# Moving two value products and the transposed maxima within each attention slot

## The chip, the core and the metric

The kernel runs on one core of a Trainium2 chip. The metric is device time in microseconds (us). Three runs of the kernel before took 499.0, 501.17 and 502.9 us (median 501.17). The profiled execution took 502.17 us, of which 500.3 us are the span that the profile covers.

## What is computed

Four batches of 512 tokens with 256 features go through a cross-attention block and then a mixture of eight experts. The attention has 16 heads of 16 features; with the causal mask only the first 512 context rows matter. The change touches the attention alone:

```python
Q = (query @ Wq.T + bq).reshape(B, Sq, H, dk).transpose(0, 2, 1, 3)
K = (key @ Wk.T + bk).reshape(B, Sk, H, dk).transpose(0, 2, 1, 3)
V = (value @ Wv.T + bv).reshape(B, Sk, H, dk).transpose(0, 2, 1, 3)
scores = jnp.einsum('bhqd,bhkd->bhqk', Q, K) / jnp.sqrt(jnp.float32(dk))
scores = jnp.where(causal, scores, -jnp.inf)
attn = jax.nn.softmax(scores, axis=-1)
out = jnp.einsum('bhqk,bhkd->bhqd', attn, V)
```

After the output projection and the residual, the feed-forward block picks two of eight experts per token and adds a shared expert. That part is not changed.

## The kernel before, in words

The program is written out engine by engine: five instruction streams, joined by semaphores, in an order that was fixed by hand. The attention works in **slots**, one for a group of four heads of a batch: 16 slots in all. The first slot has an order of its own (FIRST), then a loop runs three batches of four slots, and the last batch is written out with three slots.

A slot for head group g mixes four kinds of work on TensorE, in the order of the list SLOT. In an entry the number is that of a part.

- **R 0 to 5** (lines 624 and 626): scores of the *next* group with queries on partitions, each with a small mask product. They go to the two bank pairs of set_a. VectorE takes the row maxima from each (line 1306), and after R 5 it splits the maxima into three bfloat16 parts with four small instructions (lines 1312 to 1318).
- **MAX** (line 634): the transposed maxima of the next group, four small products from those parts into a bank of set_b. ScalarE copies the 12 rows out (line 995, function max_rows) and issues a small DMA (line 1038) that puts them beside the queries, where the next slot's S products find them.
- **S 0 to 10** (line 644): scores of *this* group with keys on partitions, already reduced by the maxima. S 0 to 3 belong to the first 128 keys, S 4 to 7 to the second, S 8 and 9 to the third, S 10 to the last. ScalarE takes the exponential of each (line 1074) into the buffers pT, and GpSimd masks the diagonal block of each key tile (line 528).
- **PV 0 to 3** (line 654): the product of the *previous* group's probabilities with the values, one part for each key tile, added up in the fourth bank of set_b. Four heads run side by side in column strips of the array. When PV 3 is done, ScalarE copies the sum out (line 995, function p_v).

Two rules set who waits. The S products and MAX share three banks of set_b in turn, so each of them may start only when the job three places before it has been read by ScalarE. The R products share two bank pairs, so each may start only when VectorE has finished with the R job two places before it. ScalarE reads the banks in the same order as TensorE fills them; p_v and max_rows stand in its stream ahead of exponential number MAX_AT.

Slots come in two kinds. In a **projection slot** (the first and third of each batch in the loop) TensorE first projects queries and keys for the next batch (line 675), VectorE first adds the biases (line 1254), and ScalarE and GpSimd split the projected values into bfloat16 parts; ScalarE does the second pair of these copies after exponential 7 (part2). In a **plain slot** (the second and fourth) none of this happens. After the fourth slot TensorE transposes the result, projects the next values and applies the output projection.

Of the kernel before, what the change touches and what calls it, by code (L numbers as in the profile page):

```python
# [44 lines left out]
def build(nc, x, ctxT, wqT, bq, wkT, bk, wvT, bv, woT, bo, gwT, wupT, wdnT, sgT, suT, sdT, out):  # L45
    B, S, D = x.shape
# [33 lines left out]
    with ExitStack() as ctx:  # L80
# [209 lines left out]
        def heads_in_bank(k):  # L290
# [21 lines left out]


        SLOT = [("R", 0), ("PV", 0), ("R", 1), ("PV", 1), ("R", 2),
                ("S", 0), ("R", 3), ("S", 1), ("R", 4), ("S", 2), ("S", 3), ("R", 5), ("S", 4), ("S", 5),
                ("S", 6), ("S", 7), ("PV", 2), ("PV", 3), ("S", 8), ("MAX", 0), ("S", 9), ("S", 10)]

        assert A_ALL % 2 == 0
        MAX_AT = 9
        FIRST = [("R", 0), ("R", 1), ("R", 2), ("S", 0), ("R", 3), ("S", 1), ("R", 4), ("S", 2), ("R", 5)]  # L320
        FIRST += [(kind, n) for kind, n in SLOT if kind == "MAX" or kind == "S" and n > 2]
        for order in (SLOT, FIRST):
# [139 lines left out]
        def _(pool):  # L462
# [38 lines left out]
            def pool_turn(signal, count):  # L501

                pool.wait_ge(signal, count)
                pool.sem_inc(pool_turns)
# [12 lines left out]
            def mask_group(n, last=False, split=None):  # L517
# [3 lines left out]
                for k in range(QT):  # L521
# [3 lines left out]
                    jobs = sum(job[0] <= k for job in S_JOBS)  # L525
                    pool_turn(b_free, n + jobs + (1 if jobs > MAX_AT and not last else 0))
                    diag = pT[k][:, :, 0:P]
# [75 lines left out]
        def _(pe):  # L603
# [25 lines left out]
            def maxima(n, par, g_count, first=False):  # L629
                pe.wait_ge(mparts_ready, g_count)  # L630
                if not first:
                    pe.wait_ge(b_free, n - 2)
                for k in range(QT):
                    last = mm(bank(par)[0:3 * HG, k * P:(k + 1) * P],
                              mparts[:, k].rearrange("p i h -> p (i h)"), identb[:], start=True, stop=True)
                last.then_inc(b_full, 1)

            def scoresT(g, j, n, par):
                pe.wait_ge(b_free, n - 2)
                k, h0, heads = S_JOBS[j]  # L640
                w = S - k * P
                for i in range(heads):
                    h = g % 2 * HG + h0 + i
                    last = mm(bank(par)[:, i * w:(i + 1) * w], kstack[0:ROWS + 3, g // 2, h, k * P:(k + 1) * P],  # L644
                              qstack[0:ROWS + 3, g // 2, h, k * P:S], start=True, stop=True)
                last.then_inc(b_full, 1)
# [63 lines left out]
            def slot(g, count, n_b, par_b, rows=None, projection=None, wait_rows=None, order=SLOT):  # L710
# [9 lines left out]
                for kind, j in order:  # L720
# [4 lines left out]
                    elif kind == "S":  # L725
                        if j == 0 and order is FIRST:
                            pe.wait_ge(b_free, B_GRP0)
                        if j == 0:
                            pe.wait_ge(max_in, DMA * (count + 1))
                        skip = 1 if rows and j >= MAX_AT else 0  # L730
                        scoresT(g, j, n_b + j + skip, par_b + j + skip)
                    elif kind == "MAX" and rows:
                        maxima(n_b + MAX_AT, par_b + MAX_AT, count + 2)

# [259 lines left out]
        def _(act):  # L994
# [38 lines left out]
            def max_rows(n, par, g):  # L1033
                act.wait_ge(b_full, n + 1)
                copy(mrows[0:3 * HG, :], bank(par)[0:3 * HG, :]).then_inc(b_free, 1)
                act.wait_ge(b_free, n + 1)
                h = g % 2 * HG
                nc.scalar.dma_start(qstack[ROWS:ROWS + 3, g // 2, h:h + HG, :], mrows[0:3 * HG, :]
                                    ).then_inc(max_in, DMA)
# [24 lines left out]
            def exps(n, par, pv=None, rows=None, split=None, down={}):  # L1064


                for j, (k, h, heads) in enumerate(S_JOBS):
                    if pv and j == MAX_AT:
                        p_v(*pv)
                    if rows is not None and j == MAX_AT:  # L1070
                        max_rows(n, par, rows)
# [17 lines left out]
            def p_v(g, count):  # L1089
                act.wait_ge(pv_full, count + 1)  # L1090
                copy(oT[:, g, :], pv_bank).then_inc(pv_free, 1)
# [553 lines left out]
```

## Time and profile before

| | |
|---|---|
| Runs | 499.0, 501.17, 502.9 us |
| Profiled execution | 502.17 us, span 500.3 us |
| TensorE busy | 458.4 us, 92% of the span |
| VectorE busy | 308.2 us, 62% |
| ScalarE busy | 210.1 us, 42% |
| GpSimd busy | 193.1 us, 39% |
| Chain that ended last | TensorE 68%, VectorE 10%, ScalarE 9%, DMA 6% |
| Mean granted TensorE clock | 0.982 of full |

The busy times are read against the span; a busy TensorE includes the tail of each matmul after its last column has been fed. In the timeline rows below the first number is the start, the second the time that the row's instructions cover, and the bracket at the end, where there is one, the idle time of the engine just before the row and what ended it. The next row's start is the better measure of what a piece of work costs in a stream.

### The profile page before, as it was taken

Reading aid. Unit: us, or ns where it says so; the run is one execution under the profiler, and the core shown is the slowest. Engines: PE = TensorE matmul, PEld = TensorE weight load, DVE = VectorE, ACT = ScalarE, POOL = GpSimd, SP = SyncE. Lnnn points to the kernel's source line nnn. Section 1 sums busy time; section 2 is a strip of 40 time slices with the busy share of each in tenths; the row PEclk is TensorE's granted clock in tenths of the full one; section 3 lists DMA queues with packets and bytes.
Section 4 is the critical chain, followed back from the end, with each engine's and each line's share of the span. In section 5 each row is a group of like instructions: output and inputs, shape, how many; then the busy total and the mean of one; then the engine's idle time right before and its main releaser. Section 6 shows DMA issues by size and latency. Waiting matters only on the chain.

```text
span 500.3 us, 10299 instructions
## 1 busy us (share of the span) xinstructions
PE 458.4 (92%) x3154; PEld 318.9 (64%) x3155; DVE 308.2 (62%) x651; ACT 210.1 (42%) x420; POOL 193.1 (39%) x204
## 2 busy tenths in 40 slices
PE   7868999999999999988699799999999999999993
PEld 6644344654447443554256366599999999999852
DVE  4984757477563757656674796855554554555436
ACT  2254666517572566517862352523322322322210
POOL 4123545114541336201512002126666766665420
PEclk9998999999999999999979899999999999999998
DMA  8593322422124121400298900014344344444279
GB/s 263 102 229 107 108 72 65 149 65 73 64 78 145 33 95 47 138 28 2 77 371 292 367 2 21 21 33 65 64 74 74 63 71 70 70 65 74 33 197 338
DMA packets 45574, 53.84 MB, mean 108 GB/s; under 512 B 7760, under 2 KB 41872, under 8 KB 44912
## 3 DMA queue, kind: packets, MB, share of 16 engines
q1 hardware_dynamic: 34320, 39.77, 24.8%
q0 software_dynamic: 7488, 10.31, 12.8%
q10 hardware_dynamic: 3744, 3.47, 2.7%
q8 instruction: 13, 0.21, 0.2%
q14 instruction: 9, 0.07, 0.1%
HBM read 27.09 MB, written 13.67 MB: 81 GB/s over the span
## 4 chain that ended last, share of the span: by engine, by line
PE 68%; DVE 10%; ACT 9%; DMA 6%; issue 5%; SPq 1%; DVEq 0%; ACTq 0%; POOLq 0%
PE set_a L624 7%; PE set_b L654 7%; PE set_a L924 6%; PE set_a L925 5%; PE set_a L923 5%; ACT attention L1074 5%; PE set_a L851 5%; PE set_a L675 4%; PE set_b L644 4%; DVE attention L1306 3%; PE set_b L861 3%; PE set_b L942 3%; PE set_a L832 3%; PE set_b L943 3%; PE set_b L944 3%
## 5 line engine op out<-in xcount | busy, mean ns | idle before, releaser
L1306 DVE TENSOR_REDUCE attention<-set_a 128x2 f32<-128x1024 f32 (+2 forms) x96 | 95.9, 1042 | 28.0 <-PE set_a L626 26.1
L1074 ACT ACTIVATE attention<-set_b 128x512 f32<-128x512 f32 (+1 forms) x176 | 88.4, 570 | 58.5 <-PE set_b L644 45.8
L528 POOL TENSOR_SCALAR_AFFINE_SELECT attention<-attention 128x512 f32<-128x512 f32 x64 | 40.8, 650 | 110.4 <-ACT attention L1074 110.4
L588 POOL DMA_INDIRECT sum_rows<-moe,token_of x39 | 61.8, 1585 | 43.9 <-issue 28.9
L644 PE MATMUL set_b<-attention 99*128 99x512 bf16 (+3 forms) x256 | 60.4, 310 | 13.6 <-ACT attention L1074 10.2
L624 PE MATMUL set_a<-attention 96*128 96x512 bf16 (+3 forms) x256 | 61.5, 306 | 5.6 <-DVE attention L1306 5.4
L580 POOL DMA_INDIRECT e_x<-normed_rows,token_of x39 | 39.4, 1010 | 63.7 <-DVE token_of L1504 37.3
L1173 ACT ACTIVATE moe<-set_a 128x384 f32<-128x384 f32 x39 | 19.1, 490 | 104.9 <-PE set_a L925 104.9
L1529 DVE TENSOR_TENSOR moe<-set_a,moe 128x384 f32<-128x384 f32 x39 | 21.8, 558 | 62.7 <-ACT moe L1173 62.7
L624 PEld LDWEIGHTS set_a<-attention 96*128 96x128 bf16 x256 | 25.3, 99 | 45.3 <-DVE attention L1306 18.0
L923 PE MATMUL set_a<-wup_hi,e_xT_hi 128*128 x156 | 53.1, 340 | 0.0
L924 PE MATMUL set_a<-wup_lo,e_xT_hi 128*128 x156 | 52.9, 339 | 0.0
L925 PE MATMUL set_a<-wup_hi,e_xT_lo 128*128 x156 | 52.8, 338 | 0.0
L626 PE MATMUL set_a<-maskb,identb 128*128 128x128 bf16 x256 | 49.6, 222 | 0.0
L654 PE MATMUL set_b<-attention 128*32 128x128 f32 (+3 forms) x512 | 46.2, 463 | 0.4 <-ACT attention L995 0.3
L644 PEld LDWEIGHTS set_b<-attention 99*128 99x128 bf16 x256 | 19.6, 99 | 37.2 <-ACT attention L1074 24.8
L942 PE MATMUL set_b<-w_down_hi,e_hT_hi 128*128 x117 | 36.4, 311 | 1.3 <-DVE moe L1541 0.8
L995 ACT ACTIVATE attention<-set_b 12x512 bf16<-12x512 f32 (+4 forms) x48 | 25.7, 596 | 22.6 <-PE set_b L820 10.2
L509 POOL TENSOR_TENSOR attention<-attention 128x512 f32<-128x512 f32 x14 | 15.9, 1154 | 47.5 <-ACT attention L995 27.8
L944 PE MATMUL set_b<-w_down_hi,e_hT_lo 128*128 x117 | 32.9, 281 | 0.0
L943 PE MATMUL set_b<-w_down_lo,e_hT_hi 128*128 x117 | 32.9, 281 | 0.0
L995 ACT ACTIVATE attention<-attention 128x512 bf16<-128x512 f32 x32 | 19.4, 644 | 30.9 <-DVE attention L1254 26.2
(167 smaller groups left out, 843.5 us busy)
## 6 DMA issues: line engine op xcount, KB each, us to landing
attention<-attention SPq DMA_DIRECT2D x182, 64.0 KB, 2.6
wup<-in_wupT SPq DMA_DIRECT2D x2, 3072.0 KB, 14.6
sum_rows<-attention SPq DMA_DIRECT2D x2, 2048.0 KB, 13.6
wup<-sum_rows SPq DMA_DIRECT2D x8, 512.0 KB, 7.0
attention<-in_ctxT SPq DMA_DIRECT2D x7, 512.0 KB, 6.2
w_down<-in_wdnT SPq DMA_DIRECT2D x3, 1024.0 KB, 5.0
x_res<-in_x SPq DMA_DIRECT2D x4, 512.0 KB, 7.1
out<-x_res ACTq DMA_DIRECT2D x8, 256.0 KB, 4.0
```

The source lines that it names most:

```text
L588: g.indirect_dma_start(acc[i], bass.IndirectOffsetOnAxis(token_of[:, t:t + 1], 0), e_y[:, t % 2, :], None, compute_op=ALU.add).then_inc(ad ...
L624: mm(dst, qstack[0:ROWS, g // 2, h, k * P:w], kstack[0:ROWS, g // 2, h, 0:w], start=True, stop=False)
L626: last = mm(dst[:, k * P:w], identb[:], maskb[:], start=False, stop=True)
L644: last = mm(bank(par)[:, i * w:(i + 1) * w], kstack[0:ROWS + 3, g // 2, h, k * P:(k + 1) * P], qstack[0:ROWS + 3, g // 2, h, k * P:S], sta ...
L654: last = mm(pv_bank[32 * h:32 * h + 32, k * P:S], vaug[:, k, HG * g + h, :], pT[k][:, h, :], start=k == 0, stop=k == QT - 1, tile_position ...
L923: mm(dst, e_xT_hi[:, a, c, :], wup_hi[:, c, cols], start=c == 0, stop=False)
L924: mm(dst, e_xT_hi[:, a, c, :], wup_lo[:, c, cols], start=False, stop=False)
L925: last = mm(dst, e_xT_lo[:, a, c, :], wup_hi[:, c, cols], start=False, stop=c == C - 1)
L942: mm(dst, e_hT_hi[:, a, m, :], wdn_hi[:, m, cols], start=m == 0, stop=False)
L943: mm(dst, e_hT_hi[:, a, m, :], wdn_lo[:, m, cols], start=False, stop=False)
L1074: nc.scalar.activation(pT[k][:, h:h + heads, :], bank(par)[:, 0:heads * (S - k * P)], ACT.Exp).then_inc(b_free, 1)
L1306: v.tensor_reduce(dst, src, AX.X, ALU.max, negate=True).then_inc(a_free, 1)
```

## The change

The list SLOT is reordered. PV 2 goes from behind S 7 to behind S 0, PV 3 to behind S 1, and MAX from behind S 8 to ahead of it. MAX_AT goes from 9 to 8, which moves p_v and max_rows in ScalarE's stream ahead of exponential 8. FIRST is built from SLOT and so gets the new place of MAX too. No instruction is added or removed.

```diff
         SLOT = [("R", 0), ("PV", 0), ("R", 1), ("PV", 1), ("R", 2),
-                ("S", 0), ("R", 3), ("S", 1), ("R", 4), ("S", 2), ("S", 3), ("R", 5), ("S", 4), ("S", 5),
-                ("S", 6), ("S", 7), ("PV", 2), ("PV", 3), ("S", 8), ("MAX", 0), ("S", 9), ("S", 10)]
+                ("S", 0), ("PV", 2), ("R", 3), ("S", 1), ("PV", 3), ("R", 4), ("S", 2), ("S", 3), ("R", 5), ("S", 4), ("S", 5),
+                ("S", 6), ("S", 7), ("MAX", 0), ("S", 8), ("S", 9), ("S", 10)]
 
         assert A_ALL % 2 == 0
-        MAX_AT = 9
+        MAX_AT = 8
```

The first place is TensorE's stream in the first half of a slot, before the change. L644 is an S product, L624 with L626 an R product, and the rows begin with S 0; the next to last row is the first product of R 4.

```order
L644 MATMUL set_b<-attention 128x512
L617 REGISTER_ALU
L624 MATMUL set_a<-attention 128x384
L626 MATMUL set_a<-maskb,identb 128x128
L624 MATMUL set_a<-attention 128x384
L626 MATMUL set_a<-maskb,identb 128x128
L639 REGISTER_ALU
L644 MATMUL set_b<-attention 128x512
L617 REGISTER_ALU
L624 MATMUL set_a<-attention 128x256
L626 MATMUL set_a<-maskb,identb 128x128
```

The same place with the change:

```order
L644 MATMUL set_b<-attention 128x512
L652 REGISTER_ALU
L654 MATMUL set_b<-attention 32x256 x4
L617 REGISTER_ALU
L624 MATMUL set_a<-attention 128x384
L626 MATMUL set_a<-maskb,identb 128x128
L624 MATMUL set_a<-attention 128x384
L626 MATMUL set_a<-maskb,identb 128x128
L639 REGISTER_ALU
L644 MATMUL set_b<-attention 128x512
L652 REGISTER_ALU
L654 MATMUL set_b<-attention 32x128 x4
```

PV 2 (32x256) now stands between S 0 and R 3, PV 3 (32x128) between S 1 and R 4.

The second place is TensorE's stream from S 7 to the end of the slot, before the change; L634 is MAX.

```order
L644 MATMUL set_b<-attention 128x384
L652 REGISTER_ALU
L654 MATMUL set_b<-attention 32x256 x4
L652 REGISTER_ALU
L654 MATMUL set_b<-attention 32x128 x4
L639 REGISTER_ALU
L644 MATMUL set_b<-attention 128x256 x2
L630 REGISTER_ALU
L632 REGISTER_ALU
L634 MATMUL set_b<-identb,attention 12x128 x4
L639 REGISTER_ALU
L644 MATMUL set_b<-attention 128x256 x2
```

With the change:

```order
L644 MATMUL set_b<-attention 128x384
L630 REGISTER_ALU
L632 REGISTER_ALU
L634 MATMUL set_b<-identb,attention 12x128 x4
L639 REGISTER_ALU
L644 MATMUL set_b<-attention 128x256 x2
L639 REGISTER_ALU
L644 MATMUL set_b<-attention 128x256 x2
L639 REGISTER_ALU
L644 MATMUL set_b<-attention 128x128 x4
```

MAX now follows S 7 directly, and S 8, S 9 and S 10 come after it.

The third place is ScalarE's stream in a projection slot, from exponential 7 on, before the change. The rows of L995 are, in this order, the two copies of part2, p_v (128x512 out of set_b) and max_rows (12x512).

```order
L1074 ACTIVATE attention<-set_b 128x384
L1016 ISA
L995 ACTIVATE attention<-attention 128x512
L1016 REGISTER_ALU
L995 ACTIVATE attention<-attention 128x512
L1073 REGISTER_ALU
L1074 ACTIVATE attention<-set_b 128x512
L1090 ISA
L995 ACTIVATE attention<-set_b 128x512
L1034 REGISTER_ALU
L995 ACTIVATE attention<-set_b 12x512
L1038 DMA attention<-attention 3x4x512
```

With the change:

```order
L1074 ACTIVATE attention<-set_b 128x384
L1016 ISA
L995 ACTIVATE attention<-attention 128x512
L1016 REGISTER_ALU
L995 ACTIVATE attention<-attention 128x512
L1090 ISA
L995 ACTIVATE attention<-set_b 128x512
L1034 REGISTER_ALU
L995 ACTIVATE attention<-set_b 12x512
L1038 DMA attention<-attention 3x4x512
L1073 REGISTER_ALU
L1074 ACTIVATE attention<-set_b 128x512
```

Exponential 8 went behind p_v, max_rows and the DMA issue.

## Rows read from the trace of the kernel before

**Rows 1.** Stretches: length, busy of PE, PEld, DVE, ACT, POOL, clock, DMA, GB/s.
```profile
69.36:83.16 13.80, 13.01 (x95) 5.78 (x93) 8.03 (x12) 8.60 (x18) 8.04 (x8) 1.00 0.15 51
```

**Rows 2.** Waits of PE from 40 to 205 us: total, times, longest.
```profile
PE set_b L644 <- ACT attention L1074: 5.3, 17, 0.6
PE set_a L624 <- DVE attention L1306: 1.0, 6, 0.2
```

**Rows 3.** Timeline of PE, first half of a projection slot.
```profile
76.41 0.38 PE L644 MATMUL set_b<-attention 99*128 99x512 bf16 x1
76.78 0.34 PE L624 MATMUL set_a<-attention 96*128 96x384 bf16 x1
...
77.23 0.38 PE L644 MATMUL set_b<-attention 99*128 99x512 bf16 x1
77.64 0.28 PE L624 MATMUL set_a<-attention 96*128 96x256 bf16 x1
...
78.33 0.59 PE L644 MATMUL set_b<-attention 99*128 99x512 bf16 x2
78.77 0.22 PE L624 MATMUL set_a<-attention 96*128 96x128 bf16 x1
```

**Rows 4.** Timeline of PE, end of that slot; 81.00 from a narrower window.
```profile
80.54 0.86 PE L654 MATMUL set_b<-attention 128*32 128x256 f32 x16
81.00 0.40 PE L654 MATMUL set_b<-attention 128*32 128x128 f32 x8
81.33 0.39 PE L644 MATMUL set_b<-attention 99*128 99x256 bf16 x2
81.65 0.39 PE L634 MATMUL set_b<-identb,attention 128*12 128x128 bf16 x4
...
82.93 0.40 PE L644 MATMUL set_b<-attention 99*128 99x128 bf16 x4 [0.57 <-ACT attention L1074]
```

**Rows 5.** Timeline of DVE in that slot: maximum of R 4, last split.
```profile
78.53 1.23 DVE L1306 TENSOR_REDUCE attention<-set_a 128x4 f32<-128x1024 f32 x1
...
81.12 0.17 DVE L1318 TENSOR_TENSOR attention<-attention 128x16 bf16<-128x16 f32 x1
```

**Rows 6.** Timeline of ACT in that slot, in narrow windows.
```profile
80.83 0.54 ACT L1074 ACTIVATE attention<-set_b 128x384 f32<-128x384 f32 x1
81.20 1.19 ACT L995 ACTIVATE attention<-attention 128x512 bf16<-128x512 f32 x2
82.24 0.64 ACT L1074 ACTIVATE attention<-set_b 128x512 f32<-128x512 f32 x1
82.72 0.65 ACT L995 ACTIVATE attention<-set_b 128x512 f32<-128x512 f32 x1
83.19 0.57 ACT L995 ACTIVATE attention<-set_b 12x512 bf16<-12x512 f32 x1
```

**Rows 7.** Timeline of PE, then of DVE, in the plain slot ahead of it.
```profile
63.81 0.38 PE L644 MATMUL set_b<-attention 99*128 99x512 bf16 x1
64.36 0.28 PE L624 MATMUL set_a<-attention 96*128 96x256 bf16 x1 [0.17 <-DVE attention L1306]
...
68.36 0.39 PE L634 MATMUL set_b<-identb,attention 128*12 128x128 bf16 x4
69.12 0.40 PE L644 MATMUL set_b<-attention 99*128 99x128 bf16 x4
...
67.83 0.18 DVE L1318 TENSOR_TENSOR attention<-attention 128x16 bf16<-128x16 f32 x1
```

**Rows 8.** Stretches around a fall of the clock, and one without; columns as in Rows 1.
```profile
34.00:38.00 4.00, 2.21 (x16) 1.06 (x16) 2.86 (x4) 1.73 (x3) 2.99 (x3) 1.00 0.84 213
38.00:42.00 4.00, 3.63 (x20) 2.25 (x20) 1.79 (x3) 1.23 (x3) 1.53 (x2) 0.57 0.36 105
228.00:232.00 4.00, 2.63 (x32) 1.37 (x33) 0.83 (x5) 4.00 (x9) 0.94 (x2) 1.00 0.01 4
```

**Rows 9.** Timeline of PE in the last batch: S 10 of its first slot.
```profile
231.46 0.40 PE L644 MATMUL set_b<-attention 99*128 99x128 bf16 x4 [0.48 <-ACT attention L1074]
```

## Prediction, made before the run

> **What bounds the kernel now.** I began with the busy times by stretch. In a projection slot TensorE has work on it for 13.01 of 13.80 us at the full granted clock of 1.00 (2.4 GHz), VectorE for 8.03 and ScalarE for 8.60 [rows 1]. So TensorE sets the length of a slot, and a reordering of its stream can win only what it waits, and can lose by every new wait. The view of who waits for whom, over the looped attention, has the size of that: 5.3 us for exponentials ahead of S products, 1.0 us for row maxima ahead of R products [rows 2]. These are visible waits; the timeline shows more, since a wait that is shorter than a matmul's tail is not counted as idle. The reader should see in the timeline that starts, not busy times, tell the cost: S 0 starts at 76.41, an S product takes (78.77 - 78.33) / 2 = 0.22 us, so TensorE is free at 76.63 and R 3 starts only at 76.78; S 1 at 77.23 is fed by 77.45 and R 4 starts at 77.64 [rows 3]. That is 0.15 and 0.19 us of waiting for VectorE, 0.34 in all. In the plain slot it is one wait, 64.36 - 63.81 - 0.22 = 0.33 us ahead of R 4 [rows 7]. At the end of the projection slot S 10 waits 0.57 us for ScalarE [rows 4].
>
> **Price of the two moved parts.** PV 2 runs from 80.54 to 81.00 = 0.46 us, PV 3 from 81.00 to the start of S 8 at 81.33 = 0.33 us [rows 4]. PV 3 has half the columns of PV 2, so about 0.23 of its 0.33 are feed and 0.10 the change back to products of the whole array. I take the same 0.10 for the change into column strips. Behind each other the two parts pay this pair of changes once; apart, and between other products, twice. New in the first half: 0.10 + 0.46 + 0.10 for PV 2 and 0.10 + 0.23 + 0.10 for PV 3 = 1.09 us. Gone from the second half: 0.89. The extra pair is 0.20 us in each of the 15 slots that have these parts (twelve in the loop, three in the last batch). From below it is 0, if the changes hide; from above 0.32, if each costs the whole tail of a product of 128 columns: 0.22 (the last row there) [rows 3] less its feed, a quarter of the 0.22 of an S product with 512, so 0.16 a change.
> The page "TensorEngine Tiling (Array Packing)" of the Trainium skill, under Tiling Modes, Key Properties, says that changing the tiling mode drains TensorE, which speaks against splitting the pair. The rows show a smaller price, 0.10 a change; by a full drain of the size above the sum below would be some 2 us larger.
>
> **First half: what gets late.** The new work meets 0.34 us of waiting and covers it. The rest stays: 1.09 - 0.34 = 0.75 us, in a projection slot and in a plain slot alike. By that much R 4 is complete later, and S 2, S 3, R 5, S 4 and all exponentials from 2 on. It also reaches VectorE: the maximum of R 4 starts at 78.53 [rows 5], 0.20 us after TensorE went on to S 2 at 78.33 [rows 3], so VectorE is not ahead of TensorE there; it will start at 79.28, and the last split ends at 81.29 + 0.75 = 82.04 instead of 81.29 [rows 5].
>
> **Second half of a projection slot.** Before, S 7 was fed by 80.44 (PV 2 less its change), and MAX came at 81.65 with the split done at 81.29, 0.36 us of cover [rows 4, 5]. Now S 7 is fed at 80.44 + 0.75 = 81.19 and MAX could follow at once; the split is done at 82.04. PV 2, PV 3 and S 8 were the cover, and it is gone: MAX starts near 82.10 and waits some 0.85 us. What is queued behind it on TensorE are S 8, S 9 and S 10. Here I count ScalarE too. Exponential 7 starts at 80.83 + 0.75 = 81.58; the first part2 copy follows 0.37 later (81.20 - 80.83) at 81.95, both take 82.24 - 81.20 = 1.04, so p_v starts at 82.99, max_rows 0.47 later (83.19 - 82.72) at 83.46, and its 0.57 end at 84.03 [rows 6]. S 10 takes the bank that stood three jobs earlier. That was S 8 before, freed by exponential 8 at 82.24 + 0.64 = 82.88 [rows 6], and S 10 started at 82.93 [rows 4]. It is MAX's bank now, freed by max_rows, so S 10 starts at 84.03 + 0.05 = 84.08. That is **1.15 us later**: 0.75 from the first half, and 0.40 because p_v and max_rows stand where exponential 8 stood. The next slot starts behind S 10, and nothing in it can recover the loss, since TensorE runs from there without a wait through the R products.
>
> **Second half of a plain slot.** The split ended at 67.83 + 0.18 = 68.01 and MAX started at 68.36 [rows 7]; now it ends at 68.76 and MAX starts at 68.82. It completes 0.39 later [rows 4], ScalarE is through with p_v by then, max_rows takes 0.57 [rows 6], and S 10 starts at 68.82 + 0.39 + 0.04 + 0.57 + 0.05 = 69.87 instead of 69.12 [rows 7], **0.75 us later**.
>
> **What costs nothing.** The DMA of the maxima leaves sooner against the next slot's S 0, as p_v is out of its way; the masks that PV 2 and PV 3 need follow the last exponentials of the slot before, while TensorE has R 0 to R 2, PV 0, PV 1 and S 0 to do first; were they late, PV 2 would wait with R 3 and everything else behind it. SP's stream is not passed by anything; GpSimd's waits keep their order.
>
> **The sum.** Loop: 6 x 1.15 + 6 x 0.75 = 11.4 us. First slot: no value products, only S 8's 0.32 [rows 4] behind MAX instead of ahead; between 0 and 0.3, I take 0.3. Last batch: three slots whose S 10 already waits 0.48 us for ScalarE [rows 9], so part of the loss repeats; between 0 and 3 x 1.15 = 3.4, I take 1.5, as ScalarE, not the value products, sets the pace there. Together 13.2 us. Against the profiled execution, 502.17 + 13.2 = 515.4 us; that execution is 1.0 above the median of 501.17, from which it would be 514.4. With the price of an extra pair at 0 the twelve loop slots lose 12 x 0.2 = 2.4 less: 512 to 513. I say **515 us**.
>
> **Rivals.** (1) *The cover works, and it gets faster.* TensorE wins 12 x 0.34 of waits for maxima and the 0.57 ahead of S 10 in six slots: 4.1 + 3.4 = 7.5 us, about 494 us. It needs the split to be ready when S 7 has been fed, that is VectorE to end at 81.2 instead of 82.04, and p_v to find a gap ahead of exponential 8. For it: VectorE has 8 of 13.8 us of work only [rows 1]. Against it: the maximum of R 4 starts when TensorE delivers it [rows 5]. Chance 5%.
> (2) *No change within 1%.* The lateness of the first half is swallowed, since S 6 and S 7 wait for exponentials anyway; only the 0.40 for p_v and max_rows stays, in six projection slots and perhaps the last batch: 2.4 to 4 us, 504 to 506. Against it: those exponentials come later by the same 0.75. Chance 11%.
> (3) *The clock falls.* From 34 to 38 us TensorE was busy 2.21 of 4.00 us, and in 38 to 42 the mean clock was 0.57, that is 1.2 GHz for (1 - 0.57) x 2 x 4 = 3.4 us; from 228 to 232, with 2.63 busy, it stayed at 2.4 GHz [rows 8]. In my walk the last four microseconds of a projection slot hold the waits of 0.85 and 1.1 us, and their busy time lies about between these two, so I cannot exclude a fall. One takes about half of 3.4 = 1.7 us. One or two of them are inside my forecast; one in each of the twelve slots would give 12 x 1.7 = 20 us, 535. Chance of five or more, over 523: 10%.
>
> A difference under 1%, 5 us, can't be told from none here. The forecast (508 to 523) has 74%, rival 3 has 10%, rival 2 has 11%, rival 1 has 5%. So slower by over 1% has 0.84, the same 0.11, faster 0.05. The range is **507 to 524 us**: the bounds of the extra pair and the last batch (0 or 0.32, 0 or 3.4) move the sum by 5 to 6 us either way, and clock falls add on the upper side.
>
> **What the changed profile would show.** Right: R 3 and R 4 start without a wait; MAX on TensorE waits 0.5 to 0.9 us for VectorE's last split (line 1318), in every slot; S 10 waits for max_rows (line 995) instead of an exponential, over 1 us in projection slots; these grow from 13.80 to about 14.95 us and plain slots by about 0.75; VectorE shows new idle time ahead of the maxima of R 3 and R 4. Wrong, if MAX starts straight behind S 7: then VectorE keeps up and step three fails. Wrong, if S 10 still waits for an exponential: then ScalarE's order isn't the gate. If the slots are as long as forecast but the span is longer, the granted clock will show it.

## The result, and the profile after

The changed kernel takes 525.15 us (median of four runs, 524.38 to 528.79) where the kernel before takes 501.22 (499.0 to 502.9): a ratio of 1.0495, with a 95% interval of 1.0431 to 1.0558. The direction was forecast, the size was not: 515 us with a range of 507 to 524, so the loss is nearly twice the 13.2 us of the sum.

Where the time went shows best by stage. These are stretches of the kernel before, cut at the first projection slot, at the end of the loop's last slot, at the second slot of the last batch and at the first work behind its third slot. The columns are length, busy time of PE, PEld, DVE, ACT and POOL, mean granted clock, DMA share and GB/s.

```profile
45.76:208.66 162.90, 154.40 (x1169) 78.08 (x1169) 101.25 (x152) 91.78 (x186) 63.79 (x75) 1.00 0.26 84
208.66:231.70 23.04, 19.55 (x141) 12.86 (x142) 12.47 (x20) 9.02 (x18) 2.49 (x4) 1.00 0.15 53
231.70:258.04 26.34, 21.61 (x175) 9.28 (x173) 18.12 (x32) 19.64 (x37) 9.43 (x11) 0.87 0.45 149
```

The same stages of the changed kernel:

```profile
45.62:227.46 181.84, 162.17 (x1169) 78.94 (x1169) 102.37 (x152) 92.43 (x186) 63.89 (x75) 0.95 0.24 78
227.46:251.50 24.04, 19.77 (x143) 12.90 (x141) 12.56 (x20) 9.32 (x18) 2.50 (x4) 0.96 0.08 32
251.50:282.01 30.51, 24.64 (x175) 9.03 (x173) 18.50 (x32) 19.71 (x36) 9.50 (x11) 0.81 0.45 151
```

The loop grew by 18.9 us, the two stages of the last batch by 1.0 and 4.2; what lies ahead and behind changed by less than 1 us. And the clock of the loop is no longer 1.00.

Now the projection slot that answers to [rows 3, 4], from 71.27 to 86.43. First its first half on TensorE, from S 0 on (a start, then the time the row covers):

```profile
78.33 0.38 PE L644 MATMUL set_b<-attention 99*128 99x512 bf16 x1
78.63 0.64 PE L654 MATMUL set_b<-attention 128*32 128x256 f32 x8
79.20 0.34 PE L624 MATMUL set_a<-attention 96*128 96x384 bf16 x1
...
79.66 0.38 PE L644 MATMUL set_b<-attention 99*128 99x512 bf16 x1
79.97 0.43 PE L654 MATMUL set_b<-attention 128*32 128x128 f32 x8
80.33 0.28 PE L624 MATMUL set_a<-attention 96*128 96x256 bf16 x1
...
81.02 0.59 PE L644 MATMUL set_b<-attention 99*128 99x512 bf16 x2
```

Every step follows the one before without a wait, as forecast, and VectorE now has 0.36 and 0.40 us of idle time ahead of the maxima of R 3 and R 4. From the end of S 0's feed (78.55) to R 3 are 0.65 us, from that of S 1 (79.88) to R 4 0.45: 1.10 us for the two moved parts, where 1.09 were taken. S 2 starts 9.75 us after the slot began; before it was 78.33 - 69.36 = 8.97 [rows 1, 3]. The first half is late by 0.78.

Its end on TensorE:

```profile
82.58 0.72 PE L644 MATMUL set_b<-attention 99*128 99x384 bf16 x2 [0.15 <-ACT attention L1074]
84.11 0.38 PE L634 MATMUL set_b<-identb,attention 128*12 128x128 bf16 x4 [0.82 <-ACT attention L1074]
84.43 0.61 PE L644 MATMUL set_b<-attention 99*128 99x256 bf16 x4
86.03 0.61 PE L644 MATMUL set_b<-attention 99*128 99x128 bf16 x4 [0.99 <-ACT attention L995]
```

VectorE's last split and, on ScalarE in narrow windows, p_v and max_rows, which answer to [rows 5, 6]:

```profile
83.81 0.17 DVE L1318 TENSOR_TENSOR attention<-attention 128x16 bf16<-128x16 f32 x1
```
```profile
84.93 0.64 ACT L995 ACTIVATE attention<-set_b 128x512 f32<-128x512 f32 x1
85.41 0.57 ACT L995 ACTIVATE attention<-set_b 12x512 bf16<-12x512 f32 x1
```

MAX waits 0.82 us and S 10 0.99. The bracket of MAX names exponential 7 (line 1074). That is a coincidence of a few hundredths: in the rotation of three banks MAX needs exponential 5, not 7. What releases it is the split, which ends at 83.98, as e12_short_split_warm below shows. max_rows ends at 85.98 and S 10 starts at 86.03, as the walk had it.

What the walk did not carry through is the clock. First the last four microseconds of this slot and the plain slot behind it, then the plain slot ahead of it, and last the end of the loop's first projection slot:

```profile
82.43:86.43 4.00, 2.00 (x14) 1.11 (x15) 1.42 (x6) 3.54 (x9) 2.85 (x4) 0.91 0.05 17
86.43:98.30 11.87, 10.73 (x86) 4.48 (x85) 6.99 (x10) 6.45 (x13) 3.15 (x5) 0.89 0.29 94
60.65:71.27 10.62, 9.47 (x87) 4.28 (x85) 6.99 (x10) 6.45 (x13) 3.32 (x5) 1.00 0.28 92
56.65:60.65 4.00, 1.99 (x15) 0.94 (x15) 1.58 (x6) 3.71 (x9) 2.68 (x4) 1.00 0.06 18
```

In the first stretch TensorE is busy for 2.00 of 4.00 us, and its mean clock of 0.91 means that 0.7 us of it ran at 1.2 GHz: the clock fell during S 10's wait. The plain slot behind it took 11.87 us, where the undisturbed one takes 10.62. Five of the loop's six projection slots lost the clock at their end in this way, or just behind it. The first one did not, though its end is as empty (1.99).

### The profile page after: what moved, and what is told of

It reads as the page before. It is cut to its first block, busy times and chain, and to the rows that moved or that the text cites. A ratio compares the mean times of both kernels' runs of the same rounds, so it can differ in the third digit from the quotient of the medians.

```text
span 523.5 us, 10299 instructions
## 1 busy us (share of the span) xinstructions
PE 469.5 (90%) x3154; PEld 319.4 (61%) x3155; DVE 309.6 (59%) x651; ACT 210.8 (40%) x420; POOL 193.5 (37%) x204
## 3 DMA queue, kind: packets, MB, share of 16 engines
q0 software_dynamic: 7488, 10.31, 12.2%
## 4 chain that ended last, share of the span: by engine, by line
PE 67%; ACT 12%; DVE 10%; DMA 5%; issue 5%; SPq 1%; DVEq 0%; ACTq 0%; POOLq 0%
PE set_b L654 9%; PE set_a L624 8%; PE set_a L924 5%; PE set_a L925 5%; PE set_a L923 5%; ACT attention L1074 5%; ACT attention L995 4%; PE set_a L675 4%; PE set_b L644 4%; PE set_a L851 3%; PE set_b L942 3%; PE set_a L832 3%; PE set_b L943 3%; PE set_b L944 3%; PE set_b L933 2%
## 5 line engine op out<-in xcount | busy, mean ns | idle before, releaser
L1306 DVE TENSOR_REDUCE attention<-set_a 128x2 f32<-128x1024 f32 (+2 forms) x96 | 97.1, 1043 | 50.3 <-PE set_a L626 49.6
L1074 ACT ACTIVATE attention<-set_b 128x512 f32<-128x512 f32 (+1 forms) x176 | 86.7, 567 | 80.9 <-PE set_b L644 80.7
L644 PE MATMUL set_b<-attention 99*128 99x512 bf16 (+3 forms) x256 | 58.9, 312 | 17.7 <-ACT attention L995 8.9
L624 PE MATMUL set_a<-attention 96*128 96x512 bf16 (+3 forms) x256 | 65.3, 321 | 4.0 <-DVE attention L1306 4.0
L624 PEld LDWEIGHTS set_a<-attention 96*128 96x128 bf16 x256 | 25.9, 101 | 50.8 <-DVE attention L1306 19.5
L654 PE MATMUL set_b<-attention 128*32 128x128 f32 (+3 forms) x512 | 55.2, 515 | 1.0 <-ACT attention L995 1.0
L626 PE MATMUL set_a<-maskb,identb 128*128 128x128 bf16 x256 | 51.0, 227 | 0.0
L644 PEld LDWEIGHTS set_b<-attention 99*128 99x128 bf16 x256 | 20.6, 100 | 40.0 <-ACT attention L1074 17.0
L995 ACT ACTIVATE attention<-set_b 12x512 bf16<-12x512 f32 (+4 forms) x48 | 26.8, 606 | 22.2 <-PE set_b L820 10.4
L995 ACT ACTIVATE attention<-attention 128x512 bf16<-128x512 f32 x32 | 19.5, 644 | 31.5 <-DVE attention L1254 29.8
```

The costliest lines, as they stand in the source:

```text
L624: mm(dst, qstack[0:ROWS, g // 2, h, k * P:w], kstack[0:ROWS, g // 2, h, 0:w], start=True, stop=False)
L626: last = mm(dst[:, k * P:w], identb[:], maskb[:], start=False, stop=True)
L654: last = mm(pv_bank[32 * h:32 * h + 32, k * P:S], vaug[:, k, HG * g + h, :], pT[k][:, h, :], start=k == 0, stop=k == QT - 1, tile_position ...
L995: copy = lambda o, i: nc.scalar.activation(o, i, ACT.Copy)
L1074: nc.scalar.activation(pT[k][:, h:h + heads, :], bank(par)[:, 0:heads * (S - k * P)], ACT.Exp).then_inc(b_free, 1)
L1306: v.tensor_reduce(dst, src, AX.X, ALU.max, negate=True).then_inc(a_free, 1)
```

## The experiments

All times stand beside runs of the kernel before on the same chip (medians 501.2, 502.1 and 502.18 us in the three sets).

### The two halves of the change: e1_pv_only and e2_max_only

```diff
-                ("S", 0), ("R", 3), ("S", 1), ("R", 4), ...
-                ("S", 6), ("S", 7), ("PV", 2), ("PV", 3), ("S", 8), ("MAX", 0), ...
+                ("S", 0), ("PV", 2), ("R", 3), ("S", 1), ("PV", 3), ("R", 4), ...
+                ("S", 6), ("S", 7), ("S", 8), ("MAX", 0), ...
```

> The kernel before with only the two value products moved; MAX stays behind S 8 and p_v and max_rows ahead of exponential 9. Theory (two gates at the end of the slot, both fed by the late first half, and clock falls after the waits they make): the first half is late by 0.75 us as in the change, MAX waits about 0.6 us for VectorE's split behind S 8 instead of 0.85, S 10 waits for exponential 8 and is 0.7 late in projection slots and 0.3 in plain ones: 7 us of waits, and some clock falls, so 508 to 515 us. Rival (the new place of MAX and of the two copies is what costs): 501 to 503 us. Rival (the split pair of value products drains TensorE, so the whole loss is theirs): 520 us or more.

Measured 516.75 us, ratio 1.032 (1.024 to 1.040). Projection slots take 14.6 us (+0.8). Of the plain slots those without a fall take 10.4; the one behind each batch's first projection slot takes 11.67, and the clock is at 1.2 GHz at that point in all three batches. So the moved value products alone make most of the loss. The undisturbed slots are as long as its 7 us of waits give; the time came out above the upper end of what was expected because of the clock.

```diff
-                ("S", 6), ("S", 7), ("PV", 2), ("PV", 3), ("S", 8), ("MAX", 0), ("S", 9), ...
+                ("S", 6), ("S", 7), ("PV", 2), ("PV", 3), ("MAX", 0), ("S", 8), ("S", 9), ...
-        MAX_AT = 9
+        MAX_AT = 8
```

> The kernel before with only MAX moved ahead of S 8 and p_v and max_rows ahead of exponential 8; the value products stay between S 7 and MAX. Theory: the cover of MAX stands, it does not wait for the split; S 10 waits for max_rows and is 0.4 us late in projection slots and about 0.1 in plain ones; no new clock falls: 504 to 506 us. Rival (MAX's new place is what costs): 515 us or more. Rival (order on ScalarE is of no matter): 501 us.

Measured 503.25 us, ratio 1.0047 (1.0021 to 1.0073), a little less than expected. Projection slots take 14.21 us (+0.4) and plain slots 9.93 (+0.17), as the walk gives for S 10 behind max_rows, and no fall of the clock is in the loop. PE's waits from 45 to 212 us:

```profile
PE set_b L644 <- ACT attention L995: 7.3, 12, 1.0
PE set_b L644 <- ACT attention L1074: 1.7, 11, 0.2
```

The wait for exponentials [rows 2] has become one for max_rows. MAX does not wait at all: with PV 2 and PV 3 ahead of it its cover stands.

### The clock: e3_keep_warm, e10_warm_s10, e11_warm_max

The first edit stands in the function of MAX, the second in the slot; the lines between are left out.

```diff
 maxima:
+                    for _ in range(12):
+                        mm(bank(par)[:, 0:P], identb[:], beforeb[:], start=True, stop=True)
                 pe.wait_ge(mparts_ready, g_count)
 slot, ahead of S 10 in projection slots:
+                            pe.wait_ge(a_free, rows[0] + ahead - 1)
+                            for _ in range(14):
+                                mm(pair(A, rows[1] + ahead)[:, 0, 0:P], identb[:], beforeb[:], start=True, stop=True)
```

> The changed kernel with unneeded matmuls put where TensorE waits: 12 of 128 columns ahead of MAX's wait for the split, and 14 ahead of S 10 in the loop's projection slots; they write banks that are free and are overwritten. Theory (the falls of the clock follow from these two waits): the slots wait as long as in the change, but the clock stays at 2.4 GHz in the loop, plain slots take 10.6 us instead of 12, and the time is 515 to 519 us. Rival (the falls come from something else, such as the value products in the first half): 525 us with the mean clock still at 0.96. Rival (the unneeded work delays the stream): over 525 us.

Measured 514.68 us, ratio 1.0269 (1.0215 to 1.0322): 10.5 us less than the change, with more matmuls and no wait taken away. The stages of e3, columns as above:

```profile
45.87:220.11 174.24, 168.53 (x1397) 90.67 (x1397) 102.38 (x152) 92.55 (x186) 63.92 (x75) 1.00 0.24 79
220.11:243.98 23.87, 20.24 (x155) 13.46 (x153) 12.56 (x20) 9.32 (x18) 2.50 (x4) 1.00 0.14 47
243.98:271.14 27.16, 22.37 (x187) 9.36 (x185) 18.55 (x32) 19.72 (x36) 9.50 (x11) 0.87 0.45 150
```

The loop's clock is 1.00 again and it takes 174.24 us: 11.3 more than before, none of it clock, and 7.6 less than the change, all of it clock. The last batch's second and third slots win 30.51 - 27.16 = 3.35. So the 23.2 us between the two profiled spans are 12.3 of longer slots at full clock (e3's span is 512.6; the waits and the extra changes of the value products) and 10.9 of clock.

> The changed kernel with 14 unneeded matmuls ahead of S 10 in the loop's projection slots alone. Theory (the falls in the loop need both waits of the projection slot's end): the loop has no fall or one, slots 15.0 and 10.6 us, 515 to 520 us. Rival (the wait of MAX alone makes the falls): 523 us or more.

> The changed kernel with 12 unneeded matmuls ahead of MAX alone, in every slot. Theory (the falls in the loop need both waits): no fall or one in the loop, 514 to 519 us. Rival (the wait of S 10 alone makes the falls): 521 us or more.

e10 has only the second of e3's edits, e11 only the first; each was run twice. With only one of the two waits filled the loop has no fall either: 517.83 us (1.0317, 1.0276 to 1.0359) and 514.61 us (1.0253, 1.0214 to 1.0292), projection slots 14.98 to 15.04, plain slots 10.61 to 10.63 in both. The last four microseconds of a projection slot, e10 first, then e11:

```profile
82.12:86.12 4.00, 2.78 (x29) 1.81 (x29) 1.58 (x6) 3.71 (x9) 2.68 (x4) 1.00 0.05 16
```
```profile
82.42:86.42 4.00, 2.77 (x27) 1.62 (x27) 1.58 (x6) 3.71 (x9) 2.69 (x4) 1.00 0.05 16
```

In these executions filling either wait was enough. That does not mean that a fall needs both: e6_masks_first below has lost the wait of S 10 and still falls three times in the loop. The median of e10 is 3 us above that of e11; 2.1 of that show in the last batch, where e10 fills nothing and keeps its falls (29.86 us against 27.73 for the second and third slot).

### What releases MAX: e7_short_split and e12_short_split_warm

Two instructions of the split instead of four; the maxima then have two bfloat16 parts and a third of zeros.

```diff
-                v.tensor_tensor(mrem, mneg, mparts[:, :, 0, :], ALU.subtract)...
-                v.tensor_copy(mparts[:, :, 1, :], mrem)...
-                v.tensor_tensor(mparts[:, :, 2, :], mrem, mparts[:, :, 1, :], ALU.subtract)...
+                v.tensor_tensor(mparts[:, :, 1, :], mneg, mparts[:, :, 0, :], ALU.subtract)...
```

> The kernel of e3_keep_warm (so that the clock stays out of it) with VectorE's split of the maxima in two instructions instead of four: two bfloat16 parts, the third zero, and 4 unneeded matmuls ahead of MAX instead of 12. Theory (MAX waits for the split): MAX starts 0.4 us sooner in every slot; a plain slot takes 10.2 us instead of 10.63, a projection slot stays at 15.0, since its S 10 waits for max_rows behind part2 and p_v: 511.5 to 513 us. Rival (MAX is released by exponential 7, as the profile's waits name it): 514 to 515.5 us, slots as long as in e3_keep_warm.

Measured 516.71 us (1.0293, 1.0255 to 1.0331), which is neither. The profiled execution took 903 us, and its slots can't be compared; the other four took 516.2 to 517.2 us at mean clocks of 0.976 to 0.977, where e3 has 0.982 to 0.987. So with 4 matmuls as filling the clock seems to be in the result again, and the experiment was repeated with 8:

> As e7_short_split (two instructions of VectorE's split instead of four, the third part of the maxima zero), with 8 unneeded matmuls ahead of MAX instead of 4, to keep the clock. Theory (MAX waits for the split, not for exponential 7): MAX starts 0.3 to 0.4 us sooner, plain slots take 10.2 to 10.3 us instead of 10.63, projection slots 15.0, and without falls the time is 511.5 to 513.5 us. Rival: slots as in e3_keep_warm, 514 to 515.5 us.

Measured 515.92 us (1.0279, 1.0243 to 1.0315), not faster than e3: its clock is 0.977, with a fall in the last batch that e3 lacks. But the slots answer the question. Plain slots take 10.43 us, 0.2 less than in e3, projection slots 14.99 as before. TensorE, VectorE and ScalarE at the end of a projection slot:

```profile
82.36 0.62 PE L633 MATMUL set_b<-beforeb,identb 128*128 128x128 bf16 x8
82.91 0.39 PE L636 MATMUL set_b<-identb,attention 128*12 128x128 bf16 x4
```
```profile
82.41 0.18 DVE L1321 TENSOR_TENSOR attention<-attention 128x16 bf16<-128x16 f32 x1
```
```profile
82.54 0.54 ACT L1081 ACTIVATE attention<-set_b 128x384 f32<-128x384 f32 x1
```

MAX starts at 82.91 while exponential 7 runs until 83.08, so that exponential never held it. The split ends at 82.59 here, and the eight unneeded matmuls (line 633) run past that, up to MAX; that is why only 0.2 of the 0.4 us came through.

### ScalarE's queue, and where a wait goes: e4_part2_late and e6_masks_first

```diff
-                    if split is not None and (k, h + heads) == (1, HG):
+                    if split is not None and j == 8:
                         part2(split)
```

> The changed kernel with ScalarE's two part2 copies of a projection slot put behind exponential 8 instead of behind exponential 7, so that p_v and max_rows do not queue behind them. Theory: max_rows follows MAX at once, S 10 starts 0.9 us sooner in the six projection slots (5 us), MAX still waits 0.85 us, and with less waiting in one place the clock falls less often: 512 to 517 us. Rival (S 10 is late because MAX is, and ScalarE's queue is of no matter): 524 to 526 us.

Measured 524.25 us (1.0489, 1.0418 to 1.0561; four runs from 519.2 to 527.6), no gain that clears the scatter, so by its time the rival stands. The slots say otherwise: projection slots take 14.13 us instead of 15.0, the 0.9 that was expected, and plain slots behind them 11.57 instead of 10.62. The wait has moved. PE, then POOL, early in such a plain slot:

```profile
63.30 0.38 PE L644 MATMUL set_b<-attention 99*128 99x512 bf16 x1
64.59 0.64 PE L654 MATMUL set_b<-attention 128*32 128x256 f32 x8 [0.91 <-POOL attention L528]
```
```profile
61.68 2.27 POOL L514 TENSOR_TENSOR attention<-attention 128x512 bf16<-128x512 f32 x2 [2.47 <-ACT attention L995]
63.90 1.22 POOL L528 TENSOR_SCALAR_AFFINE_SELECT attention<-attention 128x512 f32<-128x512 f32 x2
```

GpSimd does part3 (line 514) ahead of the masks of key tiles 2 and 3, part3 waits for the later part2, and PV 2, now early in the slot, waits for the mask. Before, PV 2 stood late enough never to meet this. The test of it:

```diff
-                    if k == 2 and split is not None:
-                        part3(split)
... behind the loop over k:
+                if split is not None:
+                    part3(split)
```

> The kernel of e4_part2_late with one more edit: GpSimd does its last split step (part3) of a projection slot behind the masks of key tiles 2 and 3, not ahead of them. Theory (in e4 the early PV 2 waits 0.9 us for a mask that stands behind part3): that wait goes, plain slots after projection slots take 10.6 us instead of 11.6, projection slots stay at 14.1, and the time is 509 to 515 us, by how often the clock falls. Rival (PV 2 waits for something else): 519 to 525 us, plain slots 11.6.

Measured 517.84 us (1.0312, 1.0273 to 1.0351), above what was expected. The slots are as forecast: 14.14 and, where the clock holds, 10.62, and PV 2 does not wait any more. But MAX still waits 0.8 us, and at 59.7, 121.2 and 192.9 us the clock falls; a slot that it hits takes 12.2 or 15.8. By slots it should stand 5 us below e3; the clock took that back.

These falls also bound what e10 and e11 can show. First the end of the projection slot ahead of the first fall and the plain slot that it hit, then the end of the next projection slot and the plain slot behind that:

```profile
55.45:59.45 4.00, 2.86 (x26) 1.55 (x24) 2.44 (x6) 3.68 (x8) 1.27 (x2) 1.00 0.18 55
59.45:71.64 12.19, 11.04 (x87) 4.46 (x85) 6.99 (x10) 7.49 (x15) 4.75 (x6) 0.86 0.19 62
81.78:85.78 4.00, 2.85 (x25) 1.55 (x24) 2.44 (x6) 3.69 (x8) 1.27 (x2) 1.00 0.12 37
85.78:96.40 10.62, 9.47 (x87) 4.28 (x85) 6.99 (x10) 7.49 (x15) 4.74 (x6) 1.00 0.19 63
```

S 10 does not wait for max_rows here, TensorE is busier than in the stretches of e10 and e11 that kept the clock, and still the clock is lost behind one of two stretches that look the same.

### Back at the kernel before: e5, e8 and e9

```diff
 e5, in the kernel before:
-                    if split is not None and (k, h + heads) == (1, HG):
+                    if split is not None and j == 8:
                         part2(split)
```

> The kernel before with one edit: the two part2 copies of a projection slot stand behind exponential 8. Theory (there S 10 waits 0.57 us for exponential 8, which queues behind part2): S 10 starts 0.5 us sooner in the six projection slots, nothing else moves, as PV 2 stands late enough for the later masks: 497.5 to 499 us. Rival (the wait only moves to max_rows or to the masks): 500.5 to 502 us.

Measured 502.89 us (1.0015, 0.9995 to 1.0034): no change, the rival. Projection slots are 0.51 shorter (13.29), as expected, and the next slot loses 0.72 (10.47 against 9.75), for a wait that was not foreseen in this form:

```profile
85.77 1.06 PE L654 MATMUL set_b<-attention 128*32 128x512 f32 x8 [0.65 <-ACT attention L995]
```

PV 0 of the next slot needs p_v to have emptied the fourth bank, and p_v now queued behind part2.

> The kernel of e5_before_part2 with unneeded matmuls in the first slot (12 ahead of R 2, 16 ahead of S 0) and in the last batch's third slot (4 ahead of each of S 2 to S 7), where TensorE waits and the clock of the kernel before falls. Theory (a fall costs about half of the 3.4 us at 1.2 GHz where TensorE has work): the falls near 38 and 250 us go, and it is 1 to 4 us faster than e5_before_part2: 494 to 497.5 us. Rival (TensorE only waits in those stretches anyway): as e5_before_part2, within 0.7 us.

The kernel has 28 unneeded matmuls in the first slot and 24 in the last. Measured 502.71 us (1.0016, 0.9998 to 1.0034), the same as e5: the rival. The falls near 38 and 250 us were gone (one stands at 28.6 instead), the mean clocks are 0.986 to 0.996 against 0.975 to 0.987 in e5, and by the medians nothing was won. So in the first slot and in the last batch's third, where TensorE waits for others, the slow clock cost nothing that could be measured; in the loop it has work, and a fall cost about 1.5 us.

```diff
 e9, in the kernel before: part2 behind p_v and max_rows, ahead of exponential 9
-                    if split is not None and (k, h + heads) == (1, HG):
-                        part2(split)
...
+                    if split is not None and j == MAX_AT:
+                        part2(split)
                     act.wait_ge(b_full, n + 1)
```

> The kernel before with the two part2 copies of a projection slot put behind exponential 8, p_v and max_rows, ahead of exponential 9. Theory (in e5_before_part2 the next slot's PV 0 waited 0.65 us for p_v, which had come to stand behind part2, and so gave back what S 10 had won): S 10 starts 0.5 us sooner in six projection slots, PV 0 does not wait, and the time is 497.5 to 499.5 us. Rival (another wait takes its place again): 501 to 503 us.

Measured 498.21 us, ratio 0.9923 (0.9901 to 0.9945): 0.8% faster than the kernel before, with an interval clear of 1, and within what was expected. Projection slots take 13.28, plain slots 9.76, and S 10's long wait for exponential 8 is gone from PE's waits (45 to 210 us):

```profile
PE set_b L644 <- ACT attention L1076: 1.7, 11, 0.2
PE set_a L666 <- DVE attention L1356: 1.1, 3, 0.4
PE set_a L624 <- DVE attention L1306: 1.0, 6, 0.2
PE set_a L807 <- ACT attention L995: 0.5, 3, 0.2
```

## Why the prediction was wrong

- **Price of the moved parts: right.** 1.10 us against 1.09. With the feeds of 0.46 and 0.23 taken off, a change into column strips costs 0.08 to 0.09 us and one back 0.11 to 0.13. The Trainium skill's page "TensorEngine Tiling (Array Packing)" (Tiling Modes, Key Properties) says that changing the tiling mode drains TensorE; the trace agrees that a change has a price, which stays below the 0.16 that the prediction put on a whole tail.
- **First half late by 0.75: right** (0.78), with R 3 and R 4 not waiting for VectorE any more.
- **MAX loses its cover: right.** 0.82 us of wait against 0.85, for the split. e2 shows it (with the cover MAX does not wait), and e12.
- **S 10 behind max_rows: right.** Projection slots grew from 13.84 to 15.03 (1.19 against 1.15), plain slots from 9.76 to 10.62 (0.86 against 0.75). The fourth slot of a batch grew by 0.55 only, since p_v is early enough for the transposes behind it, which before waited 0.17 us for ScalarE (at 93.24). e4 shows the queue at work: with part2 behind exponential 8 the projection slot is 0.9 us shorter.
- **The sum of waits: right, with some luck.** 11.4 us were taken for the loop and 1.5 for the last batch. e3 measures 11.3 and 0.83 + 0.82 = 1.65; it runs in 514.7 us, and the sum from the median was 514.4. The loop's figure is this close because errors cancel: three plain slots grew by 0.86 and three by 0.55, where 0.75 was taken for all six. The 0.3 us for the first slot did not show (45.62 us up to the loop, before 45.76).
- **The range: added up wrongly.** Its two named bounds move the sum by at most 4.5 us down (15 x 0.20 + 1.5) and 3.7 up (15 x 0.12 + 1.9), not by 5 to 6 either way. The rest of the room up to 524 was for about three falls of the clock.
- **The clock: this step failed.** The sum has no term for falls of the clock. The prediction held them as a rival, with "One or two of them are inside my forecast" and 10% for five or more. There were five in the profiled loop and more in the last batch. The price of a fall, 1.7 us, was about right: the loop's 7.6 us are 1.5 for each. Its number was not. The prediction had seen that the two waits fall into the same four microseconds, and compared that stretch with one that lost the clock, 2.21 of 4.00 busy, and one that kept it, 2.63 [rows 8]. It put the new stretch between them. But its own two waits leave 4.00 - 0.85 - 1.1 = 2.05, below both, and the stretch measured 2.00. By its own comparison a fall should have been the likely case in each projection slot, and the forecast 514.4 + 6 x 1.7, some 525 us. That the waits brought the falls on is shown by e3, e10 and e11: with the waits filled and the slots as long, the loop keeps its clock. That 525 is so near to the measured time is partly luck, since some 3 us of the loss are falls in the last batch.

Which of such stretches loses the clock stays open. TensorE's busy time in it does not decide alone: the changed kernel kept the clock once at 1.99 of 4.00 us, and e6 lost it behind 2.86, where e10 and e11 kept it at 2.78 and 2.77. The falls also differ from run to run (spans of 522.5 to 526.9 us at mean clocks of 0.964 to 0.947).

## What to carry to other kernels

Before work is moved forward on an engine that is nearly full, ask what it had been covering: here the moved 0.9 us had covered VectorE's last step, and everything behind it came late. When a walk finds new waits on TensorE that a loop repeats, put falls of the clock into the sum, priced from a row, and not only among the rivals; add up what is left of TensorE's work in the stretch with the walk's own figures, and set it beside stretches of the same trace that lost and that kept the clock. That comparison tells what is likely and no more, as the open point above shows. To find the price of a fall, fill the wait with unneeded matmuls, as e3 does. And in a cycle of engines that feed each other, look behind each wait that is removed for the next one in line (e4, e5). In e9 p_v and max_rows no longer stand behind the two copies, and the exponentials that do made no new wait: plain slots keep their 9.76 us.

## What was not expected of the hardware

- Waits can cost a second time through the clock: about 2 us of waiting at the end of a projection slot, none of the waits longer than 1.0 us, led to 1.2 to 1.6 us more in the slot behind it.
- Matmuls without use can pay where TensorE waits anyway: 264 of them, 228 in the loop, made the changed kernel 10.5 us faster, at undisturbed slots as long as without them (10.63 against 10.62). They are free only while they end before the wait does; in e12 they outlast it.
- In the kernel before, falls in the first slot and in the last batch's third cost nothing that could be measured (e8 against e5: 502.71 against 502.89 us at a higher clock). In the changed kernel's last batch they did cost: its second and third slot take 30.51 us, and 27.16 in e3.
- In the loop MAX starts 0.13 us after the split's end (84.11 against 83.98); ahead of the loop it starts 0.06 us after it (44.12 against 44.06). In the loop the code waits on a count in a register and ahead of it on a constant; no run shows whether that is the reason.
